# Graph attention and expert FFN: the edge stage's program as a loop over sixteen groups instead of one straight run of all 224

## The reference

```python
# x (6250, 256), src and dst (100000,), sorted by dst, edge_weight (100000,)
xn = layernorm(x)
x_l, x_r = xn @ W_l + b_l, xn @ W_r + b_r                 # 8 heads of 32
g = leaky_relu(x_r[dst] + x_l[src], 0.2)
alpha = einsum('ehc,hc->eh', g, att) + log(edge_weight)
ex = exp(alpha - segment_max(alpha, dst)[dst])
alpha = ex / (segment_sum(ex, dst)[dst] + 1e-16)
x = x + segment_sum(x_l[src] * alpha, dst) + bias
xn = layernorm(x); idx = top_k(xn @ Wg + bg, 2)
x = x + sum over both experts e of gelu(xn @ W1[e] + b1[e]) @ W2[e] + b2[e]
```

## Time and profile before

| | before |
|---|---|
| time, median of 3 runs (lowest, highest) | 1942.67 us (1942.07, 1944.47) |
| the profiled execution's own time | 1944.47 us |
| its span in the profile | 1942.8 us |
| mean granted TensorE clock | 0.937 |
| TensorE matmul, weight load busy | 1707.9, 1450.3 us |
| VectorE, ScalarE, GpSimd busy | 1467.7, 1247.9, 1213.6 us |
| `edges`: first gather to last add | 175.4 to 1340.6 us |

### The profile page before, as it was taken

How to read it: one execution, slowest core, us unless ns; L and a number is a source line. 1 busy time by engine, 2 the same in 40 slices (tenths; PEclk the granted TensorE clock), 3 DMA queues, 4 the chain that set the end, 5 groups by cost and what they waited for, 6 DMA issues and landing times. The chain is left out here.

```text
span 1942.8 us, 35858 instructions
## 1 busy us (share of the span) xinstructions
PE 1707.9 (88%) x9397; PEld 1450.3 (75%) x9398; DVE 1467.7 (76%) x2732; ACT 1247.9 (64%) x3160; POOL 1213.6 (62%) x1338
## 2 busy tenths in 40 slices
PE   4785689999999999999999999994977999999950
PEld 3664578878887887888878787873967999999940
DVE  6683689989999999999999999997884334333425
ACT  2353479989999999999999999884711333333310
POOL 3675777777777777777777777732455555555510
PEclk9897899999999999999999999998578999999975
DMA  6678777878778787878777778743802222222229
GB/s 227 158 230 262 215 241 236 244 225 240 238 241 240 237 242 237 239 245 242 236 239 241 237 245 240 237 133 121 300 20 71 71 70 70 70 70 70 70 90 333
DMA packets 217937, 372.87 MB, mean 192 GB/s; under 512 B 45061, under 2 KB 103661, under 8 KB 217597
## 3 DMA queue, kind: packets, MB, share of 16 engines
q1 hardware_dynamic: 157217, 214.44, 33.6%
q0 software_dynamic: 52992, 147.92, 27.1%
q10 hardware_dynamic: 7564, 8.65, 1.3%
HBM read 316.77 MB, written 55.32 MB: 192 GB/s over the span
## 5 line engine op out<-in xcount | busy, mean ns | idle before, releaser
L798 POOL DMA_INDIRECT rows<-left_rows,idx x880 | 841.9, 957 | 272.4 <-issue 267.9
L1128 PE MATMUL p_row<-rights,hotT 128*128 128x256 f32 x1760 | 503.9, 368 | 54.5 <-issue 27.5
L1130 PE MATMUL p_row<-rows,ident 128*128 128x256 f32 x1760 | 529.9, 383 | 0.0
L1191 PE MATMUL p_gain<-W,hots 128*128 128x264 f32 x1760 | 473.6, 393 | 9.3 <-DVE acc L983 7.5
L1128 PEld LDWEIGHTS p_row<-rights,hotT 128*128 128x128 f32 x1760 | 322.1, 192 | 130.4 <-issue 81.4
L1191 PEld LDWEIGHTS p_gain<-W,hots 128*128 128x128 f32 x1760 | 324.3, 190 | 83.3 <-issue 20.5
L1018 ACT ACTIVATE L<-p_row 128x512 f32<-128x512 f32 x440 | 259.4, 590 | 129.3 <-PE p_row L1130 126.9
L954 DVE TENSOR_TENSOR W<-rows,p_weights 128x1024 f32<-128x1024 f32 x220 | 267.0, 1214 | 48.5 <-PE p_gain L1191 45.8
L1088 ACT ACTIVATE far<-iota_row,dl 128x128 f32<-128x128 f32 x880 | 299.2, 391 | 0.0
L1617 ACT ACTIVATE e_hT<-e_ph,b_column 128x128 f32<-128x128 f32 x420 | 120.0, 368 | 267.3 <-PE e_ph L1642 267.3
L863 DVE TENSOR_TENSOR L<-L,p_weights 128x1024 f32<-128x1024 f32 x220 | 266.1, 1210 | 27.8 <-ACT L L1018 27.8
(11 more groups left out here) (244 smaller groups left out, 1918.1 us busy)
## 6 DMA issues: line engine op xcount, KB each, us to landing
rights<-right_rows SPq DMA_DIRECT2D x440, 256.0 KB
locals<-item_locals SPq DMA_DIRECT2D x110, 256.0 KB, 3.8
rows<-left_rows,idx POOLq DMA_INDIRECT x880
right_rows<-p_parts SPq DMA_DIRECT2D x49, 256.0 KB
c_rows<-results SPq DMA_DIRECT2D x12, 1024.0 KB, 13.5
w<-in_L_ffn_W SPq DMA_DIRECT2D x16, 512.0 KB, 6.5
left_rows<-p_y SPq DMA_DIRECT2D x49, 132.0 KB
kept_rows<-X SPq DMA_DIRECT2D x7, 896.0 KB, 4.8
```

Of the source, the lines that this page charges most:

```text
L798: nc.gpsimd.indirect_dma_start(out=rows[:, g.slot(RINGS), n, :], out_offset=None, in_=d["left"][:, :], in_offset=bass.IndirectOffsetOnAxis ...
L1128: nc.tensor.matmul(to, hotT[:, g.slot(2), i, :], rights[:, g.slot(2), n, part * D:(part + 1) * D], start=(part == 0), stop=False)
L1130: last = nc.tensor.matmul(to, s["ident"][:, :], rows[:, g.slot(RINGS), i, 0:D], start=False, stop=True)
L1191: last = nc.tensor.matmul(p_gain[:, n, 0:D + H], hots[:, g.slot(2), i, :], W[:, g.slot(2), i, :, :].rearrange("p h c -> p (h c)"), start=( ...
```

## The change

All five calls of `pipeline` in `edges` pass `un` = `2 * TURN` = 16 instead of 224. The loop then runs over `i` = 1 to 12: groups 16 to 207 are twelve passes through one body of sixteen groups, groups 0 to 15 and 208 to 223 stay straight code. The new argument `unrolled` keeps the last `TURN` groups out of the loop on GpSimd, SyncE and TensorE, whose stages have no offset that would do so, since the groups from 220 on are idle and can only be left out where `g.n` is a number. Inside the body each wait's value and each address that depends on `g.n` is worked out in registers. The operations on data, their order and their buffers are the same.

```diff
--- before.py
+++ after.py
@@ -106,7 +106,7 @@
         eng.wait_ge(sem, value)
 
 
-def pipeline(eng, steps, stages, un=UN):
+def pipeline(eng, steps, stages, un=UN, unrolled=0):
 
     most, least = max(a for a, _ in stages), min(a for a, _ in stages)
 
@@ -117,7 +117,7 @@
                 stage(g)
 
     first = max(1, -(least // un))
-    turns = max(first, (steps - max(most, 0)) // un)
+    turns = max(first, (steps - max(most, unrolled)) // un)
     for c in range(-most, first * un):
         at(0, c)
     if turns > first:
@@ -800,7 +800,7 @@
                             in_offset=bass.IndirectOffsetOnAxis(ap=idx[:, parity(g), at:at + 1], axis=0),
                         ).then_inc(gathered[r], 16)
 
-                pipeline(pool, GROUPS, [(0, live(gather))], GROUPS)
+                pipeline(pool, GROUPS, [(0, live(gather))], 2 * TURN, TURN)
 
             @block.sync
             def _(sp):
@@ -831,7 +831,7 @@
                                          d["marks"][kind * QI * P:(kind + 1) * QI * P, :][bass.ds(k * CHUNK, CHUNK), :]
                                          .rearrange("(b u) e -> b (u e)", b=BLOCKS)).then_inc(marks_in[r], 16)
 
-                pipeline(sp, GROUPS, [(1, live(load_rights)), (4, live(load_locals)), (6, load_chunk)], GROUPS)
+                pipeline(sp, GROUPS, [(1, live(load_rights)), (4, live(load_locals)), (6, load_chunk)], 2 * TURN, TURN)
 
             @block.vector
             def _(v):
@@ -983,7 +983,7 @@
                         nc.vector.tensor_tensor(to, to, p_gain[:, n, 0:D + H], ALU.add).then_inc(added, 1)
                     return stage
 
-                list_sources(Step(0, 0, GROUPS))
+                list_sources(Step(0, 0, 2 * TURN))
                 v.wait_ge(keys_spread, 1)
                 nc.vector.tensor_copy(key_of[:, :, :], p_row[:, 0, 0:2 * CHUNKS].rearrange("p (a k) -> p a k", a=2)
                                       ).then_inc(matched, 1)
@@ -1004,7 +1004,7 @@
                 pipeline(v, GROUPS, [(0, live(scale)), (0, live(put_linear)), (0, set_open), (1 - SUM, live(add(0))), (-1, sweep), (0, live(score)),
                                      (-2, bind), (-1, sweep_back), (-2, carry_over), (TURN - 1, list_ahead), (0, empty),
                                      (-2, raise_first), (-2, raise_last), (-2, shift), (-1, set_ends), (-WEIGH, live(weigh)),
-                                     (1 - SUM, live(add(1)))], GROUPS)
+                                     (1 - SUM, live(add(1)))], 2 * TURN)
 
             @block.scalar
             def _(act):
@@ -1103,7 +1103,7 @@
                 pipeline(act, GROUPS, [(-1, keep_mark(0)), (-1, keep_mark(1)), (-1, keep_mark(2)), (1, live(part)), (0, live(rectify(0))),
                                        (1, live(one_hot)), (late, live(measure(0))), (late, live(measure(1))), (-4, exp_drop), (-3, mark_first),
                                        (0, live(rectify(1))), (-4, exp_weights), (late, live(measure(2))), (late, live(measure(3))), (-4, lower),
-                                       (late, live(mark))], GROUPS)
+                                       (late, live(mark))], 2 * TURN)
 
             @block.tensor
             def _(pe):
@@ -1196,7 +1196,7 @@
 
                 pipeline(pe, GROUPS, [(0, live(sum_rows(0))), (-2, turn), (-5, let_fall), (-SUM, live(gain(0))),
                                       (-3, spread_ends), (-4, turn_back), (0, live(sum_rows(1))), (-SUM, live(gain(1))),
-                                      (0, spread_mark(0)), (0, spread_mark(1)), (0, spread_mark(2))], GROUPS)
+                                      (0, spread_mark(0)), (0, spread_mark(1)), (0, spread_mark(2))], 2 * TURN, TURN)
 
 
 def route(nc, d, s, Wg, bg, W1, b1, W2):
```

## The result

The changed kernel takes 1972.01 us (median of 4, 1970.33 to 1978.21), the kernel before beside it 1942.37 us (median of 4, 1940.93 to 1944.47): ratio 1.0149, 95% interval 1.0136 to 1.0163. It is 29.6 us slower. The prediction said 1990 us, 1950 to 2040.

The account below looks back on a forecast made before the run. GpSimd's gather floor and a round of nearly the same length were taken to bound the kernel. Registers 19 plus back-edges 28 made 47 us, 1990 us against the median of 1942.7; range 1950 to 2040.

Parts of the forecast that it names:

- GpSimd's floor: In the steady part of `edges`, GpSimd's gathers at 1.25 us each need at least 5.00 us a group.
- the round: Weigh, gathers, TensorE's products and the weigh three groups later: 15.45 us, 5.15 a group, nearly as long as GpSimd's floor.
- What it removes, 0: Straight code of 192 groups goes; its instruction fetches were credited nothing, at most 6 us.
- Rival 3: Faster: TensorE's instruction blocks no longer compete with gathers; at most 6 us off, 1937 to 1939 us; chance 0.04.
- Registers, 19 us: Register values and separate waits behind each round's last wait add 0.30 us a round, 0.10 a group, over 192 groups.
- the round has slack that the one row hides: Lower bound of the register cost: below 0 if the round has slack or everything is computed ahead.
- Rival 2: TensorE's start delayed 0.3 to 0.66 us a group: 58 to 127 us, with back-edges 2030 to 2095 us; chance 0.10.
- Branches, 28 us: At eleven back-edges ScalarE and VectorE wait for instruction blocks, leaving 1.5 and 1.05 us idle: 2.55 x 11.
- neither is regained: With GpSimd at its floor, ScalarE's and VectorE's idle times at each back-edge both count in full, 2.55 us together.
- The engine stands until a block has come: At a back-edge, if the loop head's block is gone, a fetch takes 2.4 us, bounds 0.3 to 2.8.
- The signs named in advance: Profile after: 5.2 us a group, a longer GpSimd gap in each, holes of 1 to 2.5 us every 83 us, changed packet counts.
- Rival 4: Only one cost is real: back-edges alone 1971 us, registers alone 1962; within the forecast's range, no chance of its own.

Follow-up runs that it names:

- e8_hint: The changed kernel with a prefetch hint on the loop's branch on ScalarE and VectorE: 1942.02 us against 1940.66 for the kernel before, ratio 1.0009.
- e9_only_act: The kernel before with only ScalarE's stream looping over 16 groups, no hint, the others straight: 1958.49 us against 1939.46 for the kernel before, ratio 1.0092.
- GpSimd padded: The kernel of e8_hint with 16 more already satisfied waits a group in GpSimd's loop body: 1947.37 us against 1941.9 for the kernel before, ratio 1.0028.
- e3_rest: The changed kernel with ScalarE and VectorE straight; TensorE, GpSimd and SyncE loop: 2407.9 us against 2383.7 for the kernel before, ratio 1.0080.

## Why the prediction was right in size and wrong in half of its sum

**What bounds the kernel: right for GpSimd's floor, wrong for the round.** With the stands removed a group takes 5.02 us, close to GpSimd's 5.00; holding TensorE up behind ScalarE by 1.5 us a pass costs 1.6 us. But "whatever lengthens the round by more than a few hundredths per group lengthens the kernel" did not hold, as the step on registers shows.

**What it removes, 0: right within the error.** The hint kernel fetches 61 packets instead of 164 and is no faster (1.0009, 0.9997 to 1.0021). Rival 3, faster, has nothing left. Only the sum with the registers is measured: a gain and a cost of a few us each would look the same.

**Registers, 19 us: this is the step that failed.** The measured term is the ratio of `e8_hint`, -0.6 to 4 us with all else in it, 1.4 at the medians. The step said that what stands behind the last wait of a round lengthens every round by 0.30 us, since a sequencer can't run ahead over its wait (on GpSimd it doesn't: no group's first gather, before or after, starts sooner than 0.70 us behind the end of its wait), and it gave its own test: wrong if groups between the branches still take 5.03 us. They take 5.02 with the hint, and in the kernel after GpSimd's gaps are 0.30 us as before in most groups. The instructions are there: line 106 of the kernel after, 300 to 1200 us, where the earlier trace rows have waits alone:

```profile
L106 ACTq ALU_OP  x943: 35/35/38, 300.4 to 1199.1; - x189
L106 DVEq ALU_OP  x673: 40/40/50, 301.9 to 1199.4; - x169
```

The count was too high as well: these are 5.4 and 3.9 values a group on ScalarE and VectorE, by this line alone, where the prediction counted 10 and 9.

Why it costs nothing is in the round. The prediction let the weigh that ends at 280.99 free group 20, whose gathers start at 280.69, before that end, and explained it by rough spans. GpSimd's sequencer says otherwise. Its waits of the kernel before around 276 us, and the first gather behind the four of the earlier trace rows:

```profile
L106 POOLq EVENT_SEMAPHORE  x2: 17/2592/5168, 275.8 to 275.9; - x2
```

```profile
285.69 0.95 POOL L798 DMA_INDIRECT rows<-left_rows,idx  x1 [0.30 <-issue]
```

The long wait begins at 275.9 and ends 5.17 us later, at 281.03, just behind the weigh. The gathers that it lets through are those of the next group, and they start at 285.69, 4.7 us later, since the four of group 20 stand in the queue before them. The time between the end of the wait and the first gather of its group is the room in the round that the one row hid. Taken for every group between 300 and 1200 us, the waits and the groups paired in order, its median is 5.0 us before, 4.0 with the hint (1.9 at the least) and 2.5 in the kernel after, where it falls to 0.70 in 27 of 173 groups; 0.70 is a gather that starts at once. So the loop with its registers and short branches takes about 1 us of a room of 4.3 (5.0 less 0.7), and no time; the stands use up all of it once a pass, and then GpSimd waits. The lower bound of the step, "the round has slack that the one row hides", was the case. Rival 2 falls with it. (Its upper end is 1942.7 + 127 + 28 = 2098 us by its own sum, not 2095.)

**Branches, 28 us: right in sum, with two errors that cancel.** Between the medians of the kernel after and `e8_hint` lie 30.0 us, 28.2 when each is set against the kernel before beside it (29.6 - 1.4). The fetch was put at 2.4 us and the stand at 2.65; it is 3.5 to 4.0 us on ScalarE and 2.9 to 4.0 on VectorE. The idle holes were put at 1.5 and 1.05 us; they are 3.0 and 1.8. Then "neither is regained" was wrong: 4.8 us of holes cost 2.7. Only 1.5 of ScalarE's 3.0 us reach TensorE, about half of VectorE's 1.8 us is ScalarE's stand passed on (0.9 us in `e9_only_act`), and a part is covered by the room in the round. That too small holes, all counted, give the same sum as larger ones, half counted, is luck: 2.55 us a pass said, 2.7 measured.

**What is held.** The prediction counted bodies of 510 and 560 instructions; they are 372 and 429, and TensorE's 1,100 are 944 records. Whether the block with the loop's head is still there, which no row of before shows, the runs tell: on ScalarE and VectorE it is not, since both stand and packets come, ten a pass. That GpSimd's and TensorE's bodies are held was taken without a row for it; they stand 0.2 to 0.3 us, and TensorE's q8 has no packet in the eleven passes. Length alone is not what loses the head: with the hint the bodies of ScalarE and VectorE run their eleven passes without a packet. Without the hint the branches at 372, 429 and (GpSimd padded) 370 instructions stand, and those at 114 and, on TensorE, 944 don't. Ten packets a pass for two engines, and (94 - 37) / 11 = 5.2 a pass for the padded GpSimd, are five for each body. At the prediction's estimate of 128 instructions a packet that is 640, for bodies that would fill 2.9 to 3.4 packets: by it more is read than the body holds. That this reading goes on past the branch, and that it is what drops the head, is my inference; no run shows which packets they are. "The engine stands until a block has come" is what came to pass: in the kernel after one packet of q14 starts 1.9 to 2.4 us behind each of ScalarE's eleven branches and takes 0.3 us, and the next instruction follows 1.2 to 1.3 us behind its end, a stand of 3.5 to 4.0 us.

**The signs named in advance.** Every 83 us a hole behind `COMPARE_BRANCH`, on both engines, longer than said: yes. TensorE's packets fewer: yes, 24. The other queue "about the same": it grew by half. A longer gap on GpSimd in each group, named as a wait for the weigh: no, about two longer gaps a pass, named "issue"; the gap in each group was the register step's sign. Rival 4's first value, branches alone, 1971 us, is the result.

## What to carry to other kernels

Here the loop cost at its branch back, once a pass (2.9 to 4.0 us of stand with 372 and 429 instructions), and not in its groups (5.02 us each with the hint). In another kernel look for the first instruction behind `COMPARE_BRANCH` on each sequencer, and for the instruction queue's packets inside one pass. Where they show a refetch, try a prefetch hint on the branch (here 1972 us became 1942) or fewer passes (1950 us with four branches on each of the two engines instead of eleven); the loop with the hint is as fast as straight code here (1.0009), no faster. And before a per-round cost is added to the time, look for room in the round: how long after the wait that releases it does an operation start? A start that precedes the end of what is said to have released it is a sign that the pair is wrong.

## What was not expected of the hardware

- Behind a branch back without a hint a sequencer stood 2.6 to 4.0 us at the 1940 us level with bodies of 370 to 429 instructions, 2.9 to 4.8 us with 726 to 845, and 0.2 to 0.4 us with 114 (GpSimd) and 191 (SyncE); TensorE stood 0.3 us with a body of 944 records (410 matmuls, 410 weight loads and 124 of its sequencer).
- With the hint (`e8_hint`) no instruction packet came from 340 to 423 us, longer than a pass; without it (the kernel after), ten. The hint itself takes 31 ns on ScalarE and 39 on VectorE.
- The values for waits, (943 + 673) / 10.8 = 150 `ALU_OP` a pass on ScalarE and VectorE together by line 106 alone, didn't show in the time (`e8_hint`, with 976 + 696 `ALU_OP`: 1.0009, at most 1.0021), where the round had 4 us of room.
- The same kernel takes 1940 us in some runs and 2380 to 2415 in others, with the same chip numbers on both sides. At the slower level the operations of VectorE, ScalarE and GpSimd take as long as at the other (1243 and 1239 ns, 590 and 589, 950 and 951), TensorE's about a tenth longer (403 and 365 ns) at a granted clock of 0.88.
- A gather started 0.70 us behind the end of the wait that released it, when none was queued before it: in 27 of 173 groups of the kernel after and 87 of 124 of `e3_rest`, and in no group sooner.
